# A state-space and mixture-of-experts layer on one core: the setup block dissolved into the state-space stage

## The reference

```python
mod = (silu(c) @ wmod).reshape(4, 6, 1, 256)
sa, ca, ga, sb, cb, gb = mod[:, 0], mod[:, 1], ..., mod[:, 5]
ga = (2 * (ga >= 0) - 1) * maximum(abs(ga), 0.25)      # gb likewise
h = layernorm(x) * (1 + ca) + sa
x = x + ga * mamba(h)      # in_proj 256->1024; causal conv of 4 taps; silu; x_proj 512->64+16+16; dt_proj, softplus
                           # scan over time h = exp(delta*A)*h + (delta*u)*B, 512 channels x 16 states; y = sum(h*C)
                           # y * silu(res); out_proj 512->256
h = layernorm(x) * (1 + cb) + sb
x = x + gb * moe(h)        # top 1 of 7 routed experts by softmax, and a shared expert, each 256->1024->512->256
```

## Time and profile before

| | |
|---|---|
| median of 3 executions | 3036.81 us (3034.68 to 3037.05) |
| profiled execution | 3036.99 us, span 3035.2 |
| mean granted clock of PE | 0.831 of full speed |
| busy in the span | PE 75%, DVE 67%, ACT 44%, POOL 65% |
| HBM read, written | 106.10 MB, 39.20 MB |
| stages, from the timeline | setup to 49.7, state space from there to 1997, then shared expert, routing, routed experts |

### The profile page before, as it was taken

The page is one execution under the profiler, slowest core; times in us unless marked ns, Lnnn a source line. Parts: engine busy times, 40 slices in busy tenths (PEclk is TensorE's granted clock), DMA queues, the critical chain, the costliest instruction groups (busy, mean ns, idle before and its releaser), DMA issues. The chain is left out here.

```text
span 3035.2 us, 29143 instructions
## 1 busy us (share of the span) xinstructions
PE 2270.4 (75%) x7448; PEld 1053.1 (35%) x7449; DVE 2030.8 (67%) x2297; ACT 1321.1 (44%) x2151; POOL 1980.8 (65%) x816
## 2 busy tenths in 40 slices
PE   4677687687687786786786785349889940899998
PEld 3223233233232232232232231125555520565664
DVE  3298998998998898988988989924444440122222
ACT  1465565565565665655655655402222210222221
POOL 0189989989889889899898899900000017455553
PEclk7778788787787787787787786669999975999999
DMA  3333433433333434334333333151111100222221
GB/s 109 74 74 75 97 81 73 98 84 73 88 79 81 91 78 90 81 71 101 79 80 91 88 82 85 36 215 63 48 55 62 62 22 2 83 84 86 83 87 51
DMA packets 113435, 238.40 MB, mean 79 GB/s; under 512 B 21516, under 2 KB 75534, under 8 KB 100752
## 3 DMA queue, kind: packets, MB, share of 16 engines
q1 hardware_dynamic: 93328, 189.86, 25.7%
q0 software_dynamic: 14368, 36.00, 4.1%
q10 hardware_dynamic: 5600, 11.01, 1.0%
HBM read 106.10 MB, written 39.20 MB: 48 GB/s over the span
## 5 line engine op out<-in xcount | busy, mean ns | idle before, releaser
L721 POOL TENSOR_TENSOR hs<-hs,c_rep 128x2048 f32<-128x2048 f32 x256 | 1154.6, 4525 | 69.4 <-ACT state L560 69.2
L555 ACT ACTIVATE dA<-d_rep,a 128x512 f32<-128x512 f32 x1024 | 683.6, 686 | 621.8 <-DVE hs L641 618.0
L641 DVE TENSOR_TENSOR_SCAN hs<-dA,state,hs 128x512 f32<-128x512 f32 x768 | 914.6, 1263 | 27.1 <-ACT dA L555 25.9
L714 POOL TENSOR_TENSOR hs<-u_rep,b_rep 128x2048 f32<-128x2048 f32 x96 | 433.6, 4516 | 104.7 <-PE y_ps L437 97.4
L628 DVE TENSOR_TENSOR hs<-u_ps,b_rep 128x2048 f32<-128x2048 f32 x160 | 364.6, 2280 | 135.9 <-PE u_ps L427 135.5
L396 PE MATMUL bank<-xin,w_in 128*128 128x512 f32 x512 | 342.9, 826 | 91.2 <-ACT xpad L491 86.3
L437 PE MATMUL y_ps<-hs,gather 128*32 128x512 f32 x2048 | 275.4, 686 | 142.1 <-POOL hs L721 142.1
L407 PE MATMUL bank<-xdbl,w_dt 65*128 65x512 f32 x256 | 181.5, 847 | 174.9 <-DVE delta L617 117.8
L641 DVE TENSOR_TENSOR_SCAN hs<-dA,hs 128x512 f32<-128x512 f32 x256 | 289.8, 1202 | 12.0 <-ACT dA L555 12.0
L822 POOL TENSOR_TENSOR rstd<-var,mhalf 128x4 f32<-128x4 f32 x16 | 16.1, 1007 | 411.2 <-DVE var L924 411.2
L427 PE MATMUL u_ps<-us,spread 32*128 32x512 f32 x320 | 222.2, 782 | 72.8 <-POOL us L704 62.0
(11 more groups left out here) (169 smaller groups left out, 2646.9 us busy)
## 6 DMA issues: line engine op xcount, KB each, us to landing
d_rep<-delta SPq DMA_DIRECT2D x256, 256.0 KB, 4.3
u_rep<-us SPq DMA_DIRECT2D x384, 64.0 KB, 2.2
b_rep<-bc_rows SPq DMA_DIRECT2D x64, 256.0 KB, 4.4
c_rep<-bc_rows SPq DMA_DIRECT2D x64, 256.0 KB, 7.3
xin<-in_x SPq DMA_DIRECT2D x16, 512.0 KB, 3.8
xres<-in_x SPq DMA_DIRECT2D x16, 512.0 KB, 3.6
x<-xres SPq DMA_DIRECT2D x16, 512.0 KB, 4.4
x_sb<-x SPq DMA_DIRECT2D x16, 512.0 KB, 4.3
```

What stands on the lines that cost most here:

```text
L555: nc.scalar.activation(dA[:, u % ABANK, :], d_rep[:, q % 2, j, :], ACT.Exp, scale=t["a"][:, u:u + 1]).then_inc(da_ready, 1)
L641: nc.vector.tensor_tensor_scan(hs[:, s % RING, g, :], dA[:, u % ABANK, :], hs[:, s % RING, g, :], state[:, u:u + 1] if m else 0.0, ALU.mul ...
L714: nc.gpsimd.tensor_tensor(hs[:, s % RING], u_rep[:, i % UBUF, :].unsqueeze(1).to_broadcast([P, NG, T]), b_rep[:, par, :].rearrange("p (g t ...
L721: nc.gpsimd.tensor_tensor(hs[:, s % RING, :, :], hs[:, s % RING, :, :], c_rep[:, par, :].rearrange("p (g t) -> p g t", g=NG), ALU.mult).th ...
```

## The change

The setup block goes; its work moves into the front of the state-space stage.

- SP loads A, c, x, then wmod in two parts and the weights, each with a semaphore of its own (cw, cb, w_x and w_dt share one).
- Buffers: wmod, w_ga and the row scratch lie in ring slots 4 to 7 of `hs`, the rows in the second half of `b_rep`, w_raw and ga in that of `c_rep`. DVE and POOL wait for `scaled_stored` ahead of set 4 and set 5 of chunk 0.
- The rows ga, sb, 1+cb, gb are made once for all sequences, on 4 partitions, by four products ahead of RS 0 (`rows_ps`, in the PSUM of dA). DVE limits them with fewer instructions; SP stores 16 KB (`mod_rows`), loads ga back spread over 128 partitions, and DVE scales w_out. `shared_program` loads the rows spread over 128 partitions.
- SP stores w_out_rows behind B and C's spread and ahead of delta's, and loads w_out once it has landed.
- ACT's `silu_u(0, 0)` moves from ahead of XP to ahead of RS 0. delta*u of chunk 0 moves from POOL to DVE, and PE's first two `spread_u` ahead of the early groups.

```diff
-def setup_program(nc, ins, t, mod2_dram, gb_dram, wout_dram):
...
+            sp.dma_start(t["a"][:], ins["a_cols"]).then_inc(a_loaded, 16)
+            sp.dma_start(cT[:], ins["c"]).then_inc(c_loaded, 16)
             load_x(0)
-            load_w_out(0)
+            wmod_in = ins["wmod"].rearrange("(k p) n -> p k n", p=P)
+            sp.dma_start(wmod[:, :, 0:2 * D], wmod_in[:, :, 0:2 * D]).then_inc(cols_loaded, 16)
+            sp.dma_start(t["w_in"][:], ins["w_in"].rearrange("(k p) n -> p k n", p=P)).then_inc(w_in_loaded, 16)
...
+            sp.dma_start(wmod[:, :, 2 * D:], wmod_in[:, :, 2 * D:]).then_inc(wmod_loaded, 16)
+            sp.dma_start(w_raw, ins["w_out"].rearrange("(k p) n -> p k n", p=P)).then_inc(raw_loaded, 16)
+
+            sp.wait_ge(rows_step, 4)
+            sp.dma_start(mod_dram.rearrange("w b d -> b w d"), rows).then_inc(mod_stored, 16)
+            sp.dma_start(gb_dram, rows[:, 3]).then_inc(mod_stored, 16)
+            sp.wait_ge(mod_stored, 32)
+            sp.dma_start(ga.rearrange("p b d -> p (b d)"), mod_dram[0].rearrange("b d -> (b d)").partition_broadcast(P)).then_inc(ga_loaded, 16)
+            sp.wait_ge(ga_loaded, 16)
             sp.wait_ge(res_made, KI)
             load_x(1)
             spread_bc(0, 0)
+            sp.wait_ge(scaled, BATCH)
+            sp.dma_start(wout_dram.rearrange("b p k d -> p b k d"), w_ga).then_inc(scaled_stored, 16)
             spread_delta(0, 0)
             spread_u(0, 0, 0)
+            sp.wait_ge(scaled_stored, 16)
+            load_w_out(0)
             bodies(sp, body)
...
             for g in front:
...
+                if g == ("RS", 0):
+
+                    pe.wait_ge(wmod_loaded, 16)
+                    for i in range(2):
+                        for kc in range(KD):
+                            last = nc.tensor.matmul(rows_ps[:, 2 * i:2 * i + 2, :].rearrange("p w d -> p (w d)"), cs[:, kc, :],
+                                                    wmod[:, kc, 2 * D * (i + 1):2 * D * (i + 2)], start=(kc == 0), stop=(kc == KD - 1))
+                    last.then_inc(rows_made, 1)
...
                 group(g, -1, 0, 1)
+            spread_u(0, 0, 0)
+            spread_u(0, 1, 0)
             for g in early:
                 group(g, -1, 1, 0)
-            spread_u(0, 0, 0)
-            spread_u(0, 1, 0)
...
             for g in front:
+                if g == ("CV", 0):
+                    act.wait_ge(w_loaded, 4 * 16)
+                if g == ("RS", 0):
+                    silu_u(0, 0)
                 if g == ("XP", 0):
-                    silu_u(0, 0)
+                    act.wait_ge(selectors, 2 + NF)
...
+            dve.wait_ge(ga_loaded, 16)
+            dve.wait_ge(raw_loaded, 16)
+            for b in range(BATCH):
+                nc.vector.tensor_tensor(w_ga[:, b], w_raw, ga[:, b:b + 1, :].to_broadcast([P, KI, D]), ALU.mult).then_inc(scaled, 1)
             for j in range(KI):
                 add_delta(0, j)
+            dve.wait_ge(delta_ready, KI)
+            dve.wait_ge(us_ready, 1)
+            dve.wait_ge(xdbl_made, 1)
+            nc.vector.tensor_tensor(us[:, 0], delta[:], us[:, 0], ALU.mult).then_inc(du_ready, 1)
             layernorm(1)
...
             rsqrt(0)
-            weigh_u(0, 0)
             rsqrt(1)
...
-            sp.dma_start(mod2[:], mod2_dram).then_inc(w_loaded, 16)
+            sp.dma_start(mod2[:].rearrange("p w b d -> p (w b d)"), mod_dram[1:4].rearrange("w b d -> (w b d)").partition_broadcast(P)).then_inc(w_loaded, 16)
```

More of the change, by code:

```diff
@@ L194, in mamba_program @@
-def mamba_program(nc, ins, t, bc_dram, x1_dram, wout_dram):
+def mamba_program(nc, ins, t, bc_dram, x1_dram, wout_dram, mod_dram, gb_dram):
     x_in = ins["x"].rearrange("(c t p) d -> c p t d", t=TT, p=P)
@@ L551, in exps @@
                         act.wait_ge(scan_done, NG * NSET * c + u - ABANK + 1)
-                    elif not (known(c) and c == 0):
+                    elif known(c) and c == 0:
+                        act.wait_ge(rows_kept, 1)
+                        act.wait_ge(a_ready, 1)
+                    else:
                         last = max(v for v in range(NG * NSET) if v % ABANK == u)
@@ L627, in states_in @@
                     dve.wait_ge(bc_loaded, 16 * 2 * NF * (c + 1))
+                if known(c) and c == 0 and s == RING // 2:
+                    dve.wait_ge(scaled_stored, 16)
                 nc.vector.tensor_tensor(hs[:, s % RING], u_ps[:, i % 2, :].unsqueeze(1).to_broadcast([P, NG, T]),
@@ L708, in states_in @@
                 i = SHARED_SETS.index(s)
+                if known(c) and c == 0 and s == RING // 2 + 1:
+                    pool.wait_ge(scaled_stored, 16)
                 hold(pool, urep_loaded[i % UBUF], 16 * NF * (2 * c + i // UBUF + 1), held)
@@ L736, in body @@
                         weigh_u(c + 1, 1 - par)
+            nc.gpsimd.memset(t["mhalf"][:], -0.5).then_inc(zeroed, 1)
+            nc.gpsimd.memset(t["ident"][:], 0.0).then_inc(zeroed, 1)
+            nc.gpsimd.memset(t["gather"][:], 0.0).then_inc(zeroed, 1)
+            nc.gpsimd.memset(t["row_one"][:], 0.0).then_inc(zeroed, 1)
+            nc.gpsimd.memset(t["none"][:], 0.0).then_inc(zeroed, 1)
+            nc.gpsimd.memset(xpad[:, :, 0:KCONV - 1], 0.0).then_inc(zeroed, 1)
+            pool.wait_ge(zeroed, 6)
+            nc.gpsimd.affine_select(out=t["ident"][:], in_=t["ident"][:], compare_op=ALU.not_equal, fill=1.0,
+                                    base=0, pattern=[[-1, P]], channel_multiplier=1).then_inc(selectors, 1)
+            nc.gpsimd.affine_select(out=t["row_one"][:], in_=t["row_one"][:], compare_op=ALU.not_equal, fill=1.0,
+                                    base=-DT_RANK, pattern=[[0, 1]], channel_multiplier=1).then_inc(selectors, 1)
+            for a in range(NF):
+                nc.gpsimd.affine_select(out=t["gather"][:], in_=t["gather"][:], compare_op=ALU.not_equal, fill=1.0,
+                                        base=-DS * a, pattern=[[-1, DS]], channel_multiplier=1).then_inc(selectors, 1)
+                pool.wait_ge(selectors, 3 + a)
             rsqrt(0)
-            weigh_u(0, 0)
             rsqrt(1)
```

187 lines of the change are left out of this document (66 added, 121 removed).

## The result

The changed kernel takes 2979.36 us (median of 4 executions, 2977.4 to 2980.14) against 3036.8 before on the same chip: ratio 0.9813, 95% interval 0.9801 to 0.9825. That is 57.4 us less; 2977.5 was predicted, with 2970 to 2986 as the range. The profiled execution took 2977.4, the fastest of the four, and its span is 59.5 us shorter than before's.

The account below looks back on a forecast made before the run. The prediction took one serial chain up to the first scan, begun late behind the setup block, as the bound; 47.7 + 1.6 + 4.2 - 5.1 + 11.0 = 59.4 us off gave 2977.5, range 2970 to 2986.

Parts of the forecast that it names:

- steps 2 and 7: PE's clock at in_proj, 1.6 us gained; the shared stage's second-stage rows load, 0.
- step 1: Start of the kernel: without the setup block the first layernorm instruction comes at 5.5 instead of 53.23, 47.7 us earlier.
- The cover of the columns: Shift and scale columns ready near 10.6, first modulated eviction due at 14.1: 3.5 us spare, the thinnest cover.
- The clock, 1.6: PE at in_proj: its clock may have risen by then; bounds 0 and 3.3 us, middle taken.
- Silu and gate rows, 4.2: Ahead of x_proj: first silu before RS evictions, PE makes gate rows meanwhile; x_proj ends 4.2 us earlier, bounds 1.7 to 6.6.
- The row chain, 0: Row limits, store, ga load: ga ready at 103.8, second x issued at 106.1, 2.3 us spare, so no cost.
- The store, minus 5.1: DMA queue ahead of d_rep: storing 2.1 MB of w_out_rows at 410 GB/s delays d_rep by the full 5.1 us.
- The rival that the store overlaps the copies: DMA queue: the store uses rate the copies leave unused, 5.1 us back, 2972.4; chance 0.06.
- u_ps, plus 11.0: Before the first scan: u_ps comes ahead of chunk 1's groups, so the scan waits for d_rep and one exp alone; 11.0 gained.
- The second-stage rows, 0: Shared stage: loading 128 copies of one 12 KB row instead of a 1.5 MB table costs nothing more.
- the other reading: Shared stage: the repeated source causes the copies' half rate, so the rows' load costs 3.4 us; within a rival at 0.13.
- the rival in which it falls into another pattern: Chunk loop: engines enter with other leads, the period lengthens, slower than before; 5 us per period give 3048; chance 0.02.

Follow-up runs that it names:

- e7: Changed kernel plus seven small products on PE that nothing reads, filling its idle time ahead of in_proj: 2979.81 us, ratio 0.9811.
- e1: Changed kernel with the first silu back ahead of x_proj (XP), gate rows kept: 2982.18 us, ratio 0.9821.
- e8: Kernel before with only the first silu moved ahead of RS 0: 3032.5 us, ratio 0.9989.
- e11: Changed kernel with the store behind d_rep and u_rep, chunk 1's layernorm behind the first add of delta, spread_u behind the transposes: 2973.59 us, ratio 0.9794.
- e2: Changed kernel with the store of w_out_rows behind d_rep and u_rep instead of ahead of them: 2976.53 us, ratio 0.9801.
- e3: Changed kernel with PE's first two spread_u products back behind the early groups of chunk 1: 2985.34 us, ratio 0.9831.
- e12: Changed kernel with second-stage rows loaded from 1.5 MB that repeats nothing (wrong gates, read only up to h2T): 2979.05 us, one execution.
- e9: Changed kernel with B and C ahead of the second x, store behind u_rep, chunk 1's layernorm behind delta's first add, spread_u behind the transposes: 2976.47 us, 0.9803.
- e6: Changed kernel with B and C issued ahead of the second x and the store behind u_rep: 2976.01 us, ratio 0.9805.
- e4: Changed kernel with delta*u of chunk 0 back on POOL instead of DVE: 2978.55 us, ratio 0.9810.
- e5: Kernel before with only the shared stage's second-stage rows loaded as 128 copies of one row: 3035.7 us, ratio 1.0000.

## Why the prediction was right, step by step

The mechanism was right, and the sum with it: 59.4 against 58.8 at the first scan, 58.7 at h2T, 59.5 in the profiled span, 57.4 in the medians. Two small terms were mis-sized, steps 2 and 7. Four fifths of the sum, step 1, rest on the two timelines alone, since no run undoes it.

1. **The setup block, 47.7**: 53.23 - 5.25 = 47.98. The cover of the columns was named at 3.5 us and is 3.2.
2. **The clock, 1.6**: 0.8. The conv starts at 24.89, 73.63 - 24.89 = 48.74 earlier. The value was the middle of bounds that the rows left open, and the runs say why they do: the same instructions run in 5.1 to 6.7 us. What sets it stays open; filling the gaps ahead of it, in e7, changed nothing. That it is the clock is read from the records' lengths, eight in 5.19 us where the next eight took 3.70; the windows view gives 1.00 for the clock there (last but two of its columns) and doesn't show it:

```profile
15.00:18.20 3.20, 2.73 (x4) 1.21 (x5) 1.00 (x6) 0.32 (x1) 0.00 (x0) 1.00 0.05 17
```

3. **Silu and gate rows, 4.2**: x_proj ends at 50.43 against 103.25, 52.82 earlier, so 4.1. e1 gives 4.3 by taking the move back; e8 gives 4.9 without gate rows. The 0.8 between them is not the price of the rows alone, as e8 still loads a table ahead of the silu.
4. **The row chain, 0**: right, with more room than thought. ga is ready at 52.24 and the second x leaves at 57.57, released by PE: 5.3 us spare instead of 2.3. The seven DVE instructions took 3.4 us, not 4.8, and the store 2.1, not 3.5.
5. **The store, minus 5.1**: shown by the window at 417 GB/s and by e11, which moves it and has d_rep 5.2 us earlier (77.99 against 83.19). The Trainium skill (DMA: Bandwidth & Descriptors, "Queues, rings and completion order") has the descriptors of a ring taken in their order, and the trace agrees: 227, then 417, then 231 GB/s. The rival that the store overlaps the copies is out. e2 got only 3.1 of it in its profiled execution, for another wait stood 1.6 us behind d_rep: e11's dA comes 4.7 us after C's copies (73.28), and by that d_rep was in at 73.84 + 4.7 = 78.5 in e2, where ACT was held to 80.08.
6. **u_ps, plus 11.0**: with step 5 it made 5.9, and 58.80 - 52.82 = 6.0 were measured. Undone alone it can't take back 11.0, since with u_ps last the store lies hidden behind it: 5.9 are due. e3 shows 8.8, of which 3.0 are the clock (its transposes' eviction at 79.32 against 76.31) and 5.8 the edit; its median is 6.0 higher.
7. **The second-stage rows, 0**: right for the load, 1.0 us off for the stage. The load lands 11.1 us after its issue, where it took 10.9, so the 3.4 of the other reading is out, and most of the copies' half rate is not the repeated source's. The Trainium skill (SBUF — State Buffer, "Door 1: The DMA port swizzle") ties a transfer's rate to the ports that the written partitions reach; by it this load costs nothing more, and the two landings agree. But h2T comes 32.38 us after the issue instead of 31.36, as ACT's issues behind it are held longer. The prediction had no term for that; by e12 0.8 of it goes with the repetition, in one execution.

The loop kept its period, so the rival in which it falls into another pattern did not come about. Part of the agreement is luck: the loop's first chunks gave 0.9 us that no step had, and the shared stage lost 1.0. The median is 1.9 us above the forecast, and this can't be laid on single steps: the profiled execution has the losses of steps 2 and 7 in it and took 2977.4, while two profiled executions of the same kernel differ by 3.2 in the span (2975.7, 2978.9). The prediction called itself wrong if the end moved by another amount than the first scan. By 58.8 against 57.4 in the medians and 59.5 in the span it moved by the same as far as these executions tell.

## What to carry to other kernels

When a block ends only so that its stores land, ask which of its results the next chain reads first, and load in that order; here 48.0 of the 58.8 us at the first scan came from that. Then look behind every wait that a change removes for the next one: in this front d_rep, u_ps and chunk 1's transposes lay within 12 us of each other (71.6, 77.8 and 83.2 in the changed kernel), and in the profiled executions the store's 5 us came back in full at the first scan only when the other two were moved with it; two executions of e2, without a trace, were as fast without that. A lead at the first scan is not yet a lead at the end: e2 lost its 3.1 us again in the first chunks, and e11 kept 3.3 of 5.2. Put a store that nothing near reads behind the copies that the next instruction waits for, and put no wait for a late load ahead of work that others wait for (e9).

## What the runs showed of the hardware

- **PE's clock after a pause differs with nothing changed ahead of it.** dt_proj's last three tiles follow an idle time of 2.48 us. In the changed kernel the window 60.8 to 64.7 has a granted clock of 0.77; in e2 and e6 the same products have 0.50. From the first to the last add of delta it is 4.2 to 4.4 us in five profiled executions, 4.8 in one and 5.7 to 6.0 in six (e9 and e11 have the layernorm in between). It is not the edits: e4 and e12 change only what comes later and are among the six. In the changed kernel and its variants it goes with the start: where in_proj's first eight records took 5.1 to 5.4 us, the adds took 4.2 to 4.8, and where these took 5.8 to 6.7, the adds took 5.8 to 6.0. It doesn't in before, with 5.95 and 4.2. Together with in_proj's start this moves the front by up to 3 us, as much as some of the edits, so a single profile of one edit is read only after these two durations are compared. The windows view of e2:

```profile
61.60:67.10 5.50, 5.49 (x6) 1.79 (x6) 1.65 (x3) 4.45 (x3) 0.00 (x0) 0.50 0.74 179
```

- **One 12 KB row read 128 times** into 128 partitions, 1.5 MB beside other loads, lands as fast as 1.5 MB without repetition: 10.7 to 11.2 us in eleven profiled executions against 10.8 to 10.9 in three. Loads issued after it seem to pay 0.4 to 1.2 us (e5, e12).
- **A store among copies runs at its own rate, in its turn.** Copies into 32 partitions move at 227 and 231 GB/s and the store of 2 MB between them at 417, with a DMA share of 0.99 to 1.07 in all three windows, so the share doesn't tell the two rates apart.
